# Gate logits and expert product of the first feed-forward as one product over 520 joined columns

## The reference, cut to what matters

```
logits  = x @ W_gate.T                 # [.., 512] x [512, 8]
rw      = softmax(top2(logits))
expert  = x @ W_expert                 # [.., 512] x [512, 512]
shared  = relu(x @ W_up.T) @ W_down.T
x_out   = x_res + tanh(g_ffn[0]) * (shared + sum(rw) * expert)
```

## Time and profile before

| what | value |
|---|---|
| median of 3 runs (lowest, highest) | 1126.71 us (1125.02, 1128.56) |
| profiled execution: span from first to last instruction | 1137.7 us |
| PE busy | 1041.9 us, 92% |
| DVE busy | 681.7 us, 60% |
| POOL busy | 485.5 us, 43% |
| ACT busy | 322.6 us, 28% |
| mean granted clock of PE | 0.966 |

### The profile page before, as it was taken

The page is one execution under the profiler, slowest core; times in us unless marked ns, Lnnn a source line. Parts: engine busy times, 40 slices in busy tenths (PEclk is TensorE's granted clock), DMA queues, the critical chain, the costliest instruction groups (busy, mean ns, idle before and its releaser), DMA issues.

```text
span 1137.7 us, 16279 instructions
## 1 busy us (share of the span) xinstructions
PE 1041.9 (92%) x6109; PEld 570.0 (50%) x6110; DVE 681.7 (60%) x1290; ACT 322.6 (28%) x446; POOL 485.5 (43%) x468
## 2 busy tenths in 40 slices
PE   7988889999999999999999987789999999998586
PEld 6975544554454554545544622347555555554232
DVE  3331463778878787787788755763444444443366
ACT  3420023224133232232241321432433333333121
POOL 1100013625655665647657485054344454445100
PEclk9997999999999999999999996899999999999799
DMA  8872079579580580661603141436879999983898
GB/s 310 298 312 93 1 268 375 192 289 336 184 327 30 187 316 20 243 241 65 217 1 113 77 156 73 182 133 256 301 286 392 374 366 341 376 290 140 330 409 321
DMA packets 93786, 262.30 MB, mean 231 GB/s; under 512 B 10623, under 2 KB 10751, under 8 KB 92944
## 3 DMA queue, kind: packets, MB, share of 16 engines
q1 hardware_dynamic: 43920, 146.18, 35.1%
q10 hardware_dynamic: 31872, 63.97, 15.2%
q0 software_dynamic: 17920, 51.15, 11.5%
HBM read 129.91 MB, written 139.72 MB: 237 GB/s over the span
## 4 chain that ended last, share of the span: by engine, by line
PE 76%; DMA 7%; DVE 6%; issue 4%; ACT 3%; POOL 3%; another core or an unknown queue 1%; SPq 0%; POOLq 0%; ACTq 0%; DVEq 0%
PE banks L1178 18%; PE banks L1186 10%; PE banks L1687 10%; PE banks L1279 6%; PE banks L1319 6%; PE banks L1698 6%; DMA e_eo<-y_d 6%; PE banks L1673 6%; PE banks L1337 4%; DVE t_nmx L992 3%; PE banks L1200 2%; ACT t_probs L791 1%; PE banks L1172 1%; POOL t_psum L703 1%; PE banks L391 1%
## 5 line engine op out<-in xcount | busy, mean ns | idle before, releaser
L1526 POOL DMA_INDIRECT y_d<-e_eo,e_ids x128 | 124.5, 972 | 148.4 <-DVE e_eo L1615 117.2
L992 DVE TENSOR_REDUCE t_nmx<-banks 128x4 f32<-128x2048 f32 x64 | 146.4, 2288 | 55.0 <-PE banks L1279 54.9
L703 POOL TENSOR_TENSOR t_psum<-t_psum,t_probs 128x512 f32<-128x512 f32 x112 | 140.8, 1289 | 63.0 <-ACT t_probs L791 61.5
L791 ACT ACTIVATE t_probs<-banks 128x2048 f32<-128x2048 f32 x56 | 105.1, 1878 | 149.6 <-PE banks L1322 139.0
L715 POOL DMA_INDIRECT xs_d<-r_norm,r_xaddr x96 | 96.5, 1005 | 52.1 <-DVE r_xaddr L1125 26.5
L1279 PE MATMUL banks<-b_key,b_qry 32*128 32x512 f32 x512 | 77.1, 673 | 25.4 <-DVE t_nmx L992 19.0
L675 POOL TENSOR_TENSOR f_rstd<-f_veps,mhalf 128x2 f32<-128x2 f32 x24 | 16.9, 706 | 189.1 <-DVE f_veps L893 189.0
L1319 PE MATMUL banks<-b_qry,b_key 32*128 32x512 f32 x512 | 73.9, 647 | 16.0 <-ACT t_probs L791 7.3
L703 POOL TENSOR_TENSOR t_psum<-t_probs,t_probs 128x512 f32<-128x512 f32 x56 | 72.0, 1319 | 16.3 <-ACT t_probs L791 14.3
L1673 PE MATMUL banks<-ident,e_xg 128*128 128x128 f32 x512 | 70.4, 280 | 1.6 <-DMA e_xg<-xs_d 0.9
L1673 PEld LDWEIGHTS banks<-ident,e_xg 128*128 128x128 f32 x512 | 54.8, 141 | 26.2 <-issue 24.3
(11 more groups left out here) (217 smaller groups left out, 1653.8 us busy)
## 6 DMA issues: line engine op xcount, KB each, us to landing
xs_d<-zero ACTq DMA_DIRECT2D x32, 1056.0 KB, 9.9
e_xg<-xs_d SPq DMA_DIRECT2D x32, 1056.0 KB
y_d<-zero ACTq DMA_DIRECT2D x24, 1024.0 KB
e_xg<-y_d SPq DMA_DIRECT2D x16, 768.0 KB, 15.1
e_eo<-y_d SPq DMA_DIRECT2D x16, 768.0 KB, 14.5
wo<-in_wud SPq DMA_DIRECT2D x8, 768.0 KB
wupT<-in_wud SPq DMA_DIRECT2D x8, 768.0 KB
wdnT<-in_wud SPq DMA_DIRECT2D x8, 768.0 KB
```

The source lines that it names most:

```text
L703: ins = g_.tensor_tensor(psum0[:, q, :], first[:, q, :], probs[s % NP][:, q, :], ALU.add)
L791: A(probs[s % NP][:, :, :], quad[:, :, :], ACT.Exp, scale=SCALE1).then_inc(W["exp_ok"], 1)
L992: V.tensor_reduce(nmx[g][:, m, :], quad[:, :, :], axis=AX.X, op=ALU.max, negate=True).then_inc(W["mx_ok"], 1)
L1526: g_.indirect_dma_start(out=y_d, out_offset=bass.IndirectOffsetOnAxis(ap=ids[:, HC * p + n:HC * p + n + 1], axis=0), in_=eo[u][:, n, :], i ...
```

## The change

`wg0` (8 columns) and `wexp` (512) become one weight tile `wmix` of 520 columns per chunk, loaded by one DMA in the place of two. F.logits becomes F.mix: for each token tile the first 256 of the joined columns (8 logits and 248 of the expert), both tiles in the two halves of one bank. F.expert0/1 compute the other 264. F.weight moves ahead of F.upB (and so ahead of R.hot on DVE) and after its chain applies the 248 columns of both tiles to the residual, which raises the new semaphore `mix_ok`; it, not `gap_ok`, releases the bank. In the ending F.best moves ahead of R.sigmoid and F.weight ahead of F.upA.

```diff
-            wexp = sb("wexp", [P, KC, D], ctx=mid)
-            wg0 = sb("wg0", [P, KC, E0], ctx=mid)
+            wmix = sb("wmix", [P, KC, EX], ctx=mid)      # EX = E0 + D = 520, MIX = D // 2 - E0 = 248
...
-        weights("ffn_in", "wg0", "wupT", "wdnT", "wexp")
+        weights("ffn_in", "wmix", "wupT", "wdnT")
...  ORDER
-T.S5+1 R.x3+3 T.V0+1 F.logits+0 T.V1+1 F.best+0 T.S6+1 F.upA+0 R.sigmoid+2 T.S7+1 T.P1+1 F.upB+0 R.hot+2 T.Q2+1 F.weight+0 T.M1+1
+T.S5+1 R.x3+3 T.V0+1 F.mix+0 T.V1+1 F.best+0 T.S6+1 F.upA+0 R.sigmoid+2 T.S7+1 T.P1+1 F.weight+0 F.upB+0 R.hot+2 T.Q2+1 T.M1+1
...  ENDING
-R.x3/4 T.sum0a/6 F.logits/7 T.S7/6 R.sigmoid/5 T.sum0b/6 T.P1/6 F.upA/7 T.Q1/6 T.sum0c/6 F.upB/7 F.best/7 T.Q2/6 R.hot/5 F.weight/7 T.M1/6
+R.x3/4 T.sum0a/6 F.mix/7 T.S7/6 F.best/7 R.sigmoid/5 T.sum0b/6 T.P1/6 F.weight/7 F.upA/7 T.Q1/6 T.sum0c/6 F.upB/7 T.Q2/6 R.hot/5 T.M1/6
...  RELEASES
-    "F.logits": ("gap_ok", 1, 1),
+    "F.mix": ("mix_ok", 2, 2),
...  DVE, end of f_weight
+            x, p = xs[b % 2], halves(bank("F.mix", b))
+            for t in range(T):
+                V.scalar_tensor_tensor(out=x[:, t, 0:MIX], in0=p[:, t, E0:D // 2], scalar=rw[:, 2, t:t + 1],
+                                       in1=x[:, t, 0:MIX], op0=ALU.mult, op1=ALU.add).then_inc(W["mix_ok"], 1)
...  DVE, f_expert (f_down waits for mix_ok too)
-                V.scalar_tensor_tensor(out=x[:, t, :], in0=bank(f"F.expert{t}", b)[:, :], ...
+                V.scalar_tensor_tensor(out=x[:, t, MIX:D], in0=bank(f"F.expert{t}", b)[:, 0:D - MIX], ...
...  PE, f_mix and f_expert
-                ins = by_rows(dst[:, t * E0:(t + 1) * E0], normT, wg0, t)
+                ins = by_rows(dst[:, t, :], normT, wmix[:, :, 0:D // 2], t)
-                by_rows(open_bank(f"F.expert{t}", b)[:, :], normT, wexp, t).then_inc(W["ex_mm"], 1)
+                by_rows(open_bank(f"F.expert{t}", b)[:, 0:D - MIX], normT, wmix[:, :, D // 2:EX], t).then_inc(W["ex_mm"], 1)
```

More of the change, by code:

```diff
@@ L36 @@
 XW = D + 2 * TAG
+EX = E0 + D
+MIX = D // 2 - E0
 def decay_mask():
@@ L96, in build @@
                              iota_e=iota_e, tok_f=tok_f, tg_x=tg_x, tg_f=tg_f, comb_all=comb_all, iota_k=iota_k)
-            weights = dict(wg=wg, wo=wo, wupT=wupT, wdnT=wdnT, wexp=wexp, wg0=wg0, wg1=wg1, wsu=wsu, wsd=wsd,
+            weights = dict(wg=wg, wo=wo, wupT=wupT, wdnT=wdnT, wmix=wmix, wg1=wg1, wsu=wsu, wsd=wsd,
                            gamma=gamma, beta=beta, AT=AT, zero=zero)
@@ L143, in pair_weights @@
 def pair_weights(v):
-    flat = [v[n][:, :, :].rearrange("p k d -> p (k d)") for n in ("wo", "wupT", "wdnT", "wexp")]
+    flat = [v[n][:, :, :].rearrange("p k d -> p (k d)") for n in ("wo", "wupT", "wdnT", "wmix")]
     size = 2 * KC * 2 * HE
@@ L459 @@
     "F.gateA": ("zT_ok", 2, 1), "F.gateB": ("zT_ok", 2, 2), "F.x1a": ("x1_ok", 2, 1), "F.x1b": ("x1_ok", 2, 2),
-    "F.turn2A": ("x2T_ok", 2, 1), "F.turn2B": ("x2T_ok", 2, 2), "F.logits": ("gap_ok", 1, 1),
+    "F.turn2A": ("x2T_ok", 2, 1), "F.turn2B": ("x2T_ok", 2, 2), "F.mix": ("mix_ok", 2, 2),
     "F.upA": ("uT_ok", 2, 1), "F.upB": ("uT_ok", 2, 2), "F.expert0": ("e_ok", 2, 1), "F.expert1": ("e_ok", 2, 2),
@@ L527, in main_loop @@
     mhalf, iota_e, tok_f, tg_x, tg_f, AT = (v[n] for n in "mhalf iota_e tok_f tg_x tg_f AT".split())
-    wg, wo, wupT, wdnT, wexp, wg0, wg1, wsu, wsd = (v[n] for n in "wg wo wupT wdnT wexp wg0 wg1 wsu wsd".split())
+    wg, wo, wupT, wdnT, wmix, wg1, wsu, wsd = (v[n] for n in "wg wo wupT wdnT wmix wg1 wsu wsd".split())
     gamma, beta, comb_all, iota_k, zero = (v[n] for n in "gamma beta comb_all iota_k zero".split())
@@ L606, in main_loop @@
             "f_chain", "t_chain", "r_chain",
-            "f_var", "f_rstd_ok", "n_ok", "zT_ok", "x1_ok", "x2n_ok", "gap_ok", "e_ok", "x2_ok", "q_ok",
+            "f_var", "f_rstd_ok", "n_ok", "zT_ok", "x1_ok", "x2n_ok", "gap_ok", "mix_ok", "e_ok", "x2_ok", "q_ok",
             "mx_ok", "nmp_ok", "sum_ok", "sums_ok", "att_ok", "x3_ok",
@@ L939, in f_best @@
             dve.wait_ge(W["lg_mm"], b + 1)
-            p = bank("F.logits", b)
+            p = halves(bank("F.mix", b))
             for t in range(T):
-                ins = V.max(m8[:, t, :], p[:, t * E0:(t + 1) * E0])
+                ins = V.max(m8[:, t, :], p[:, t, 0:E0])
             link("f", ins)
@@ L958, in stage @@
                 dve.wait_ge(W["ex_mm"], 2 * b + t + 1)
-                V.scalar_tensor_tensor(out=x[:, t, :], in0=bank(f"F.expert{t}", b)[:, :], scalar=rw[:, 2, t:t + 1],
-                                       in1=x[:, t, :], op0=ALU.mult, op1=ALU.add).then_inc(W["e_ok"], 1)
+                V.scalar_tensor_tensor(out=x[:, t, MIX:D], in0=bank(f"F.expert{t}", b)[:, 0:D - MIX], scalar=rw[:, 2, t:t + 1],
+                                       in1=x[:, t, MIX:D], op0=ALU.mult, op1=ALU.add).then_inc(W["e_ok"], 1)
             return stage
@@ L966, in stage @@
                 dve.wait_ge(W["dn_mm"], 2 * b + t + 1)
+                dve.wait_ge(W["mix_ok"], 2 * b + t + 1)
                 dve.wait_ge(W["e_ok"], 2 * b + t + 1)
@@ L1238, in f_turn2, with f_mix @@
             return stage
-        def f_logits(b):
+        def f_mix(b):
             pe.wait_ge(W["x2T_ok"], 2 * b + 2)
             if b == 0:
-                pe.wait_ge(v["ffn_in"], 16 * 4)
-            dst = open_bank("F.logits", b)
+                pe.wait_ge(v["ffn_in"], 16 * 3)
+            dst = halves(open_bank("F.mix", b))
             for t in range(T):
-                ins = by_rows(dst[:, t * E0:(t + 1) * E0], normT, wg0, t)
+                ins = by_rows(dst[:, t, :], normT, wmix[:, :, 0:D // 2], t)
             ins.then_inc(W["lg_mm"], 1)
@@ L1405, in r_pos @@
             ins.then_inc(W["pos_mm"], 1)
-        stages = {"G.first": first_gate, "G.second": second_gate, "F.logits": f_logits, "T.M0": rows_of(0), "T.M1": rows_of(1), "T.Z0": sums(0), "T.Z1": sums(1),
+        stages = {"G.first": first_gate, "G.second": second_gate, "F.mix": f_mix, "T.M0": rows_of(0), "T.M1": rows_of(1), "T.Z0": sums(0), "T.Z1": sums(1),
                   "R.gates": r_gates, "R.pos": r_pos, "L.M0": rows_of(0), "L.M1": rows_of(1)}
@@ L1772 @@
         "wdnT": rows(a(L0_ffn_W_down).T),
-        "wexp": rows(a(L0_ffn_W_expert)),
-        "wg0": rows(a(L0_ffn_W_gate).T),
+        "wmix": rows(np.concatenate([a(L0_ffn_W_gate).T, a(L0_ffn_W_expert)], axis=1)),
         "wg1": rows(a(L1_ffn_w_gate)),
```

## The result

The changed kernel takes 1130.57 us (median of 20 runs, 1125.49 to 1131.97), the kernel before 1126.06 us beside it (20 runs); the ratio is 1.0032 with an interval of 1.0021 to 1.0044. One of the 20 runs of the kernel before, of 1245.04 us, stands far outside the others (1124.23 to 1129.47) and isn't in the ratio. A second measurement, further down, gives 1.0018 [0.9998, 1.0038], an interval that still includes no change. So the change doesn't pay; it seems to cost 0.2 to 0.3%. The forecast was 1128.2 us, 0.13% over.

The account below looks back on a forecast made before the run. PE's queue in program order was taken to bound the main loop. The terms -1.5 - 0.9 + 2.4 + 1.5 = +1.5 us on 1126.7 gave 1128.2 us; 8-in-10 range 1118 to 1135.

Parts of the forecast that it names:

- PE's own work: PE in each batch: mix +1.77 us against the logits, expert tiles -3.32, net -1.55 us, -12.4 over eight.
- T.M1: Main loop: M1 on PE waits for DVE to apply both halves of mix's bank, 0.57 us of new wait.
- R.pos: Main loop: PE waits 1.4 us for R.hot, whose last five small DVE operations fall into POOL's sum.
- Rival A: Main loop and ending: DVE's casts slip through between POOL instructions, only M1's wait stays; 1118.8 us, chance 0.2.
- Rival B: Main loop: R.hot waits out one POOL instruction more, its semaphore 1.23 us later; 1134.4 us, chance 0.22.
- Rival C: Whole kernel: PE's columns alone decide, all waits hidden; -12.4 us, 1114.3 us, chance 0.05.
- Steps 2 to 6: Main loop: -1.55 of PE's work, +0.57 and +1.45 of waits, +0.5 us each, +2.4 together.
- Step 1: Second step, without R.hot: M1 waits 0.5 us, Q4 starts some 0.9 us earlier; -0.9 us.
- Step 0: First step, without T or R work: expert0 follows up without a wait; -1.5 us.
- The ending: Batch 7: all seven port users of R.hot meet POOL's sum, its semaphore comes late; +1.5 us, between +0.7 and +3.
- The total: Whole kernel: +1.5 us summed over all steps and the ending, put on 1126.7, gives 1128.2 us.

Follow-up runs that it names:

- ta: The changed kernel with POOL's sum of Q2's exponentials (T.sum0b) cut to 8 of its 512 columns; 1122.47 us, ratio 0.9834.
- fb: The changed kernel with F.weight ahead of T.S7, R.sigmoid behind T.P1, R.pos, R.slots and R.places behind F.down0 (ending: behind T.V1); 1131.09 us, ratio 0.9894.
- x2: The changed kernel with joined columns and new order in batches 2 to 6 only, the others computed as before; 1129.19 us, ratio 1.0014.
- x3: The changed kernel with joined columns and new order in batch 7 only, the others computed as before; 1130.29 us, ratio 1.0020.
- g0: The changed kernel, unedited, measured again against the kernel before; 1128.08 us, ratio 1.0018.
- fa: The changed kernel with T.Q4 moved ahead of R.pos, R.slots and R.places in the steps; 1135.1 us, ratio 0.9939.
- x1: The changed kernel with joined columns and new order in batches 0 and 1 only, the others computed as before; 1124.21 us, ratio 0.9967.
- x0: The changed kernel with the joined tile and its one DMA kept, but all batches in the old columns and order; 1127.51 us, ratio 1.0008.

## Why the prediction was right, and what was mis-sized

**PE's own work: right.** 3.66 us for mix where 3.65 stood, 1.93 for an expert tile where 1.9 did.

**T.M1: right.** The chain L950 to L954 took 1.05 us (409.62 to 410.67), the pair 0.86 where I took 0.87 and the bounds were 0.72 and 1.5; the wait was 0.58, forecast 0.57.

**R.pos: right, and for the reason given.** Moved by the 5.36 us by which this step starts earlier, the forecast had R.hot at 411.48 (411.45 in the trace), POOL's sum at 413.19 (413.19), the first cast at 414.04 (414.05), the semaphore at 418.32 (418.31), Q4 at 418.62 (418.65). The wait was 1.26, forecast 1.4. One sign was not as I wrote it: I expected 1.2 us for each of the five small operations; the first took 0.49 and the last 0.21, as they began late in a POOL instruction or between two (the last at 418.10, between the sums' instructions of 416.87 and 418.27). What counts is where the chain ends, and that follows from POOL's boundaries. `ta` shows the cause. Rival A needed the casts to slip through; they don't. Rival B needed 0.36 us more ahead of the first cast; nothing was late by more than 0.1. Rival C would hold only without the waits; not even `fb`, with both removed, reaches it.

**Steps 2 to 6: right.** +2.4 us forecast, +0.53 in each of the five, +2.65.

**Step 1: right.** -0.9 forecast, -0.8 measured (75.5 to 74.7).

**Step 0: sign right, size wrong.** -1.5 forecast; like with like -3.3 measured in the shorter executions (51.4 to 48.1) and -2.4 to -3.5 in the longer. PE in step 0, before:

```profile
99.26 3.58 PE L1178 MATMUL banks<-wg,f_normT 128*128 128x8 f32 x16 [0.69 <-ACT f_normT L763]
102.69 9.73 PE L1186 MATMUL banks<-f_normT,wupT 128*128 128x256 f32 x32
112.26 7.03 PE L1178 MATMUL banks<-wexp,f_normT 128*128 128x512 f32 x16
```

and after:

```profile
97.31 5.91 PE L1184 MATMUL banks<-wmix,f_normT 128*128 128x256 f32 x16 [0.69 <-ACT f_normT L764]
103.06 7.07 PE L1192 MATMUL banks<-f_normT,wupT 128*128 128x256 f32 x32
109.97 3.72 PE L1184 MATMUL banks<-wmix,f_normT 128*128 128x264 f32 x16
```

I used prices at the upper clock level for a place where it is, at first, at the lower. The logits run at 0.50 throughout, mix for its greater part (granted clock 0.50 from 95 to 100 us and 0.82 from 100 to 105): it costs 2.3 us more than the logits (5.75 against 3.43, start to start). But the upper level is back sooner after: up takes 6.91 us where it took 9.57. From the first row's start to the expert's end that is -3.65 (2.32 - 2.66 - 3.31). The kernel before had one of the longer steps 0, but in `x2`, of the shorter kind, the same three groups take 19.9 us as well. Why the clock rises sooner isn't settled.

**The ending: right for the part that I worked out.** Mix to L.S0 takes 43.1 us in four executions with the new ending (`x3`, `g0` and the two others of the changed kernel; a fifth, `fa`, has 3.9 us of PE's idle time without a releaser in it), and 40.4 to 42.1 in the six with the old one beside that of the kernel before: +1.0 to +2.7, forecast +1.5 (0.7 to 3). The timeline in the changed kernel:

```profile
646.71 5.59 POOL L704 TENSOR_TENSOR t_psum<-t_probs,t_probs 128x512 f32<-128x512 f32 x4 [7.84 <-ACT t_probs L792]
647.50 2.43 DVE L1087 TENSOR_TENSOR r_onehot<-iota_e,r_norm 128x384 bf16<-128x384 f32 x2
...
651.52 0.86 DVE L1091 CAST r_chosen<-r_chosen 128x128 bf16<-128x128 f32 x1
...
...
654.04 0.20 PE L1409 MATMUL banks<-r_chosen,before 128*128 128x64 bf16 x1 [2.31 <-DVEq L1097]
```

As forecast the whole of R.hot meets POOL's sum; R.pos waits 2.3 us where it had 1.4 to spare. What the forecast lacks is the clock: right behind this wait it is low for a while, in the changed kernel (the first two rows: window, busy times as above, clock, DMA) and in the five others with R.pos in that place, while `x1`, at about the same stages with the old ending (last row), keeps it at 1.00:

```profile
650.00:655.00 5.00, 2.69 (x20) 1.79 (x22) 4.70 (x10) 2.33 (x2) 4.86 (x4) 0.97 0.01 2
655.00:660.00 5.00, 5.00 (x25) 1.12 (x16) 4.78 (x7) 1.88 (x1) 4.39 (x5) 0.69 0.00 0
...
650.00:655.00 5.00, 5.00 (x24) 1.60 (x16) 4.75 (x7) 1.88 (x1) 4.86 (x5) 1.00 0.00 0
```

`x0`, with the old ending, has such a low window (0.66) at 645 to 650 us and takes 42.1 us, the four others of 40.4 have none. `fb`, whose R.pos stands later and waits 0.9 us, has none there either. So about 1.7 us of the 2.7 are the clock's and 1.0 the order's. That the wait brings the low clock on is argued from the order of events, not shown.

**The total.** Two errors work against each other: step 0's gain was forecast 1.8 us too small, and the ending had no clock term, of up to 1.7 us. That the sum came out near is in part luck. With the measured terms, step 0 at -3.3, the sum is -3.3 - 0.8 + 2.65 + (1.0 to 2.7) = -0.5 to +1.3 us. The two comparisons have +3.6 us [2.4, 5.0] and +2.0 [-0.2, 4.3]; the lowest runs differ by 1.3 (1125.49 - 1124.23) and 1.9 (1125.88 - 1124.00). So some 2 to 4 us of the first comparison are outside my terms. The long stretch of low clock is the size for it, if it comes more often after the change than before: 16 of the 20 runs there took 1129.7 us or more, in the second comparison 5 of 12 took 1130.9 or more. That it does come more often is argued, not shown, and a long time doesn't need it, as `x0` at 1132.73 us shows.

## What to carry to other kernels

When PE's work is made cheaper in a full pipeline, write down the times at which each following stage becomes due and the semaphore it meets; here 1.55 us of PE per batch became +0.53, and the loss was in the order of another engine's queue. A change that moves a DVE chain should be looked at for what POOL does at its new time: three of five tiny operations grew from 0.2 to between 1.16 and 1.34 us. Then try the edit with the delayed chain moved as well; with that, and batch 7 left as it was, a 0.2 to 0.3% loss became a 0.56% gain.

## What the runs showed of the hardware that was not expected

- The same program reaches the same point at 691.4 us and then takes 35.8 or 40.6 us, by how long the granted clock stays at 0.50 there. The 20 runs of the changed kernel also fall into two groups (1125.5 to 1127.4 and 1129.7 to 1132.0 us); that this stretch makes the groups isn't shown.
- Step 0 with the same stages takes 48.1 or 50.4 to 50.7 us (old tiles: 51.4 or 53.1 to 53.9), by a low clock that does or doesn't fall on a product ahead of them (8.80 us or 7.1).
- DVE's operations with a PSUM source weren't lengthened by POOL's sum. The pair of 264 columns (L964) took this beside it, against 0.86 for the 248 columns (L957) with POOL idle:

```profile
418.87 0.89 DVE L964 SCALAR_TENSOR_TENSOR f_xs<-banks,f_rw,f_xs 128x264 f32<-128x264 f32 x2
```

The Trainium skill ("SBUF — State Buffer", SBUF: two separate sides) puts the longer operations down to a pair of ports that VectorE and GpSimd can't hold at once: the instruction that starts first has it to its end, and the other waits. The rows agree: 1.27, 1.34 and 1.16 us beside POOL instructions of 1.26 us, 0.2 beside the thinned one, and 0.89 for the pair that reads PSUM.
